# An attention layer and a routed expert layer on one core: two sends in flight, u before v, block 7's rotation after the experts

## The chip, the cores and the metric

One core of a Trainium2 chip runs the whole program. The metric is the device time of one launch in microseconds (us): three runs before, with a median of 402.08 (401.18 to 405.04). A profile was taken of one more execution.

## The reference

The input x has 8 batches (here called blocks, b = 0 to 7) of 512 rows of 128 numbers. Both branches read the normalized rows xn, and their results are added to x.

```python
xn = layernorm(x)                                   # outer one, without weights
# attention branch: its own layernorm on xn, with weights, gives y
uv = silu(y @ uv_w.T + uv_b); u, v, base = uv[..., :256], uv[..., 256:512], uv[..., 512:]
q, k = rope(base * gamma + beta)                    # two versions of base, each rotated
kernel = square(relu(q @ k.T / sqrt(128) + bias[distance]))
attn = (u * (kernel @ v)) @ o_w.T + o_b + xn
# expert branch: 4096 rows, 8 experts, each row goes to its best 2
probs = sigmoid(xn @ W_router); top 2, divided by their sum
ffn = sq_relu(xn @ W_sh_up) @ W_sh_down + sum over the 2 experts of weight * sq_relu(xn @ W_up[e]) @ W_down[e]
out = x + attn + ffn
```

## The kernel before, in words

Five engines run programs of their own and meet at semaphores; each executes its instructions in the order written. **Blocks 0 to 6** run first, one `turn` each, then the **experts**, then **block 7** by one more `turn`, then the results of the experts are added to all blocks (`combine`) and stored. A float32 product of full precision is made of three faster ones: each operand is split in a high half (a copy in a rounded type, by ScalarE) and a low half (the difference, by VectorE), and `product` (lines 1009 to 1011) multiplies low by high, high by low and high by high.

A turn of TensorE holds, for its block: v (`v_part`, four products of 256 columns for each half), two of the four parts of the shared expert's first layer (`shared_up`), the gate products u (`uv_part` by `gates`), the scores (`scores`, four), the other two shared parts, the shared second layer (`shared_down`), `values` (kernel times v, four), and among them the output product and the transposition of the block before (`output`, `output_turned`), and the transposed rows and the base products of the block after. In block 0 the gates come first and v last.

**Banks.** These products share a ring of four PSUM banks. `RING` lists its users in the order in which TensorE issues them, and `ring_free` makes TensorE wait until the user four places earlier has been read out. What counts as read out stands in `READ`: for v that VectorE has added v's bias, for u that ScalarE has applied SiLU (`u_silu`, line 495), for a shared part ScalarE's ReLU, for a score VectorE's first pass of the kernel square (line 782). In blocks 1 to 7 u's two banks are those that v's two halves had.

**VectorE's turn** (line 815): the gating u * (kernel @ v) of the block before (`gate`, line 793), `v_bias` (line 773), `qk_split` (line 767), four kernel squares (lines 782 and 785), the next block's norm, then the low halves and the rotation of the next block: `rotate_base` (lines 753 and 756) needs ScalarE's base_qk (line 482), `rotate_sum` (line 762) adds the two products. **ScalarE's turn** (line 513): first it waits for the rotated sum and copies its high half (qk_hi, line 515); then come the shared ReLUs, `v_silu` (line 490), `u_silu`, the squares, and the next block's base. `u_silu` also waits until the gating of the block before has read u.

**Routing.** In blocks 0 and 1 the rows of all eight groups are transposed (`routing_turned`), copied by ScalarE (`routing_copied`, line 455) and multiplied by the router's weights (`routing_logits`). Group g's logits wait for its copy. VectorE picks the two best in block 1, and in block 2 counts and places the rows (`routing_counts`, `routing_slots`). At the end of block 1 it makes the weights of the two experts (`routing_weights`, lines 703 to 709).

**Sends.** From block 2 on GpSimd issues 64 indirect DMAs (line 987), each of which writes 128 rows of 130 numbers to the slots of their experts in DRAM (`slots_in`). `IN_FLIGHT` is the number of semaphores (lanes) that they use in turn: a send waits for the landing of the send that had its lane before. SP loads W_up during the blocks (line 359), then W_down (line 370), then waits for all sends (line 374), and loads the slots' rows in pairs of tiles (line 378). There are 72 tiles of 128 slots. TensorE starts the experts when block 6 is added up (`mixed`) and the first pair of tiles has landed; the steps are paced by TensorE and results go back by GpSimd (line 996). Block 7 starts on TensorE when VectorE has made the last tile's result (line 911).

Of the kernel before, what the change touches and what calls it, by code (L numbers as in the profile page):

```python
# [67 lines left out]
def build(nc, x, ln_w, ln_b, uv_w, uv_b, gamma, beta, w, o_w, o_b,  # L68
# [10 lines left out]
    with ExitStack() as ctx:  # L79
# [111 lines left out]
        ld_w = [sem(f"ld_w{i}") for i in range(ROUNDS)]  # L191
        ld_wdn = sem("ld_wdn")
        zero_filled = sem("zero_filled")
        IN_FLIGHT = 2 * TOPK
        tokens_sent = [sem(f"tokens_sent{k}") for k in range(IN_FLIGHT)]
        zeros_set = sem("zeros_set")

# [52 lines left out]
        RING = [("x1", 0), ("x2", 0), ("base", 0), ("bsw", 0), ("rt", 0)]  # L250
        for b in range(B):
            values, up, gates, rt = [("v0", b), ("v1", b)], [("sh0", b), ("sh1", b)], [("u0", b), ("u1", b)], [("rt", g) for g in range(B)]
            if b == 0:
                RING += gates + up + values
            elif b == 1:
                RING += values + [rt[5], up[0], rt[6], up[1]] + gates + [rt[7]]
            else:
                RING += values + up + gates
            RING += [("qk0", b), ("qk1", b), ("qk2", b), ("qk3", b), ("sh2", b), ("sh3", b)]
            RING += [("fin", b - 1)] if 0 < b < LAST else []  # L260
            if b == 0:
                RING += [rt[1], ("x2", 1), rt[2], ("base", 1), ("bsw", 1), rt[3], ("x1", 1), rt[4]]
            elif b < LAST:
                RING += [("x2", b + 1), ("base", b + 1), ("bsw", b + 1), ("x1", b + 1)]
            if b >= LAST - 1:
                RING += [("fin", b)]
# [137 lines left out]
        def _(act):  # L404
# [46 lines left out]
            def routing_copied(g):  # L451
                act.wait_ge(ring_ready, ready("rt", g))
                if g >= 2:
                    act.wait_ge(logits_made, g - 1)
                act.copy(route_xt[g % 2].rearrange("p t d -> p (t d)"), ring("rt", g)[:, :]).then_inc(rx_copied, 1)
# [29 lines left out]
            def v_silu(b):  # L485
                for n in range(2):
                    act.wait_ge(v_biased, START + b * 2 + (n + 1))
                    act.wait_ge(av_done, START + b * TB)
                    part = vf[:, 2 * n:2 * n + 2, :].rearrange("p t e -> p (t e)")
                    act.activation(v[:, 2 * n:2 * n + 2, :].rearrange("p t e -> p (t e)"), part, ACT.Silu).then_inc(v_made, 1)  # L490

            def u_silu(b):
                act.wait_ge(g_made, START + b * 2)
                for n in range(2):
                    act.activation(ut[:, n, :], of_ring(f"u{n}", b), ACT.Silu, bias=uvbias[:, n:n + 1])\
                       .then_inc(ut_made, 1)
# [6 lines left out]
            def shared_square(b, c):  # L503
                act.wait_ge(sh_relu, START + b * HC + (c + 1))
                act.activation(sh[:, c % 2, :], sh[:, c % 2, :], ACT.Square).then_inc(sh_made, 1)
# [7 lines left out]
            def turn(b, first, last, route):  # L513
                act.wait_ge(qk_made, START + b + 1)
                act.copy(qk_hi[:, :, :].rearrange("p a t -> p (a t)"),
                         rot1.rearrange("p a t -> p (a t)")).then_inc(qk_hi_made, 1)
                if route == 1:
                    routing_copied(5)
                shared_relu(b, 0)
                if route == 1:  # L520
                    routing_copied(6)
                shared_relu(b, 1)
                v_silu(b)
                if not first:
                    u_silu(b)
                if route == 1:
                    routing_copied(7)
                shared_square(b, 0)
                shared_square(b, 1)
                if 0 < b < LAST:  # L530
                    output_out(b - 1)
                if route == 1:
                    routing_probs()
                if 3 <= route < LAST:
                    weights_hi(2 * route - 5)
                    weights_hi(2 * route - 4)
                shared_relu(b, 2)
                shared_relu(b, 3)
                if route == 0:
                    norm(1)  # L540
                    norm(2)
                    routing_copied(1)
                if not last:
                    second_rows_hi(b + 1)
                shared_square(b, 2)
                shared_square(b, 3)
                if route == 0:
                    norm(3)
                    norm(4)
                    routing_copied(2)  # L550
                if not last:
                    base_silu(b + 1)
                    if route == 0:
                        routing_copied(3)
                    first_rows_hi(b + 1)
                if route == 0:
                    routing_copied(4)
                    norm(5)
                    norm(6)
                    norm(7)  # L560
# [46 lines left out]
        def _(dve):  # L607
# [156 lines left out]
            def qk_split(b):  # L764
                dve.wait_ge(qk_hi_made, b + 1)
                dve.wait_ge(qk_made, START + b + 1)
                dve.tensor_tensor(qk_lo[:, :, :], rot1, qk_hi[:, :, :].bitcast(F32), ALU.subtract).then_inc(qk_lo_made, 1)  # L767
# [20 lines left out]
            def gate(b):  # L788
                dve.wait_ge(out_acc, START + b)
                for n in range(2):  # L790
                    dve.wait_ge(av_done, START + b * TB + TB)
                    dve.wait_ge(ut_made, START + b * 2 + (n + 1))
                    dve.tensor_tensor(g[:, n, :], P_AV[n][:, :], ut[:, n, :], ALU.mult).then_inc(g_made, 1)
# [21 lines left out]
            def turn(b, first, last, route):  # L815
                if 0 < b < LAST:
                    gate(b - 1)
                v_bias(b)
                qk_split(b)
                if route == 0:  # L820
                    statistics(2, 12, 20)
                    dve.wait_ge(ld["bias"], 16)
                kernel_square(b, 0)
                kernel_square(b, 1)
                if route == 0:
                    variances(slice(FIRST, 20))
                elif not last:
                    second_norm(b + 1)
                kernel_square(b, 2)
                kernel_square(b, 3)  # L830
                if route == 0:
                    second_norm(1)
                    statistics(3, 20, NT)
                if route == 1:
                    routing_first()
                if route == 2:
                    routing_counts()
                if route == 3:
                    routing_owners()
                if 3 <= route < LAST:  # L840
                    weights_lo(2 * route - 5)
                if not last:
                    second_rows_lo(b + 1)
                if 0 < b < LAST:
                    mix(b - 1)
                if route == 0:
                    variances(slice(20, NT))
                if route == 1:
                    routing_second()
                if route == 2:  # L850
                    routing_tiles()
                    routing_slots()
                if 3 <= route < LAST:
                    weights_lo(2 * route - 4)
                if not last:
                    rotate_base(b + 1)
                    first_rows_lo(b + 1)
                    rotate_sum(b + 1)
                if route == 1:
                    routing_weights()  # L860

            first_norm(0)
            second_norm(0, True)
# [61 lines left out]
            expert_steps(dve, step)  # L925


            turn(LAST, False, True, LAST)
            for b in (0, 1, 2):
                combine(b)  # L930
# [72 lines left out]
        def _(pe):  # L1003
# [132 lines left out]
            def turn(b, first, last, route):  # L1136
# [4 lines left out]
                def first_up():  # L1141
                    pe.wait_ge(x1_lo_made, START + b + 1)
                    if first:
                        pe.wait_ge(w_lo_made, 1)
                    shared_up(b, 0)
                    if route == 1:
                        routing_turned(6)
                    shared_up(b, 1)

                if first:  # L1150
                    gates()
                    first_up()
                v_part(b, 0)
                v_part(b, 1)
                if first:
# [1 line left out]
                    pe.wait_ge(ld["wr"], 16)  # L1157
                    routing_logits(0)
                if route == 1:
                    routing_logits(4)  # L1160
                    routing_turned(5)
                if not first:
                    first_up()
                    gates()
                if route == 1:
                    routing_logits(5)
                    routing_turned(7)
                    routing_logits(6)
                if route == 2:
                    routing_counted()  # L1170
# [147 lines left out]
```

## Time and profile before

| | us |
|---|---|
| median of 3 runs | 402.08 |
| profiled execution, own time | 402.41 |
| its span | 400.6 |
| mean granted TensorE clock | 0.977 |
| TensorE / ScalarE / VectorE / GpSimd busy | 366.8 / 238.3 / 230.9 / 154.0 |

The span begins with the first instruction and ends with the last; the own time holds what lies around it too. Blocks 0 to 6 take about the first 210 us, the experts end at 371, and block 7 and the sums take the rest. All times named below are counted from the span's start. A line of a timeline has start, duration, engine, source line, operation, what is written and read, how many such instructions follow one another, and in brackets how long the engine had been idle and whose result ended that. The bank names of TensorE have no numbers, and `work` holds many buffers: the source line tells which is meant.

### The profile page before, as it was taken

The page shows a single profiled execution, that of the slowest core. Times are in us where ns is not written, and L with a number is a line of the kernel's source. Part 1 is how long each engine was busy: PE and PEld are TensorE (multiplying, and loading weights), DVE is VectorE, ACT ScalarE, POOL GpSimd, SP SyncE. Part 2 cuts the span into 40 slices and gives each one's busy share as a digit, 9 for nine tenths or more (in the row PEclk, how much of TensorE's full clock was granted, in tenths as well). Part 3 has the DMA queues.
Part 4 walks back from the last instruction along what each step waited for, and adds up shares of the span by engine and source line. Part 5 has one row for each costly group of instructions (what it writes and reads, how often), then busy time and mean ns, then how long its engine had stood idle before and what let it go on. Part 6 is the DMA issues. An engine that isn't in the chain of part 4 may idle for free.

```text
span 400.6 us, 7289 instructions
## 1 busy us (share of the span) xinstructions
PE 366.8 (92%) x1966; PEld 278.8 (70%) x1967; DVE 230.9 (58%) x594; ACT 238.3 (59%) x447; POOL 154.0 (38%) x155
## 2 busy tenths in 40 slices
PE   1779899969989999999968999999999999999991
PEld 1565586556555656656526999999999999999740
DVE  3888458778986867858562333334334334333676
ACT  0765994752565746666434666666666676676420
POOL 3004600000277877776500344444444434445100
PEclk9989999989999999999996999999999999999997
DMA  6999000000012122156111122222222222221596
GB/s 158 316 291 272 15 2 0 0 2 0 7 47 82 58 80 75 47 145 209 49 27 28 55 56 60 67 60 60 65 62 60 58 62 66 62 64 33 152 298 200
DMA packets 50594, 34.53 MB, mean 86 GB/s; under 512 B 6032, under 2 KB 46864, under 8 KB 50576
## 3 DMA queue, kind: packets, MB, share of 16 engines
q1 hardware_dynamic: 44256, 23.77, 23.5%
q0 software_dynamic: 4352, 8.99, 6.7%
q10 hardware_dynamic: 1968, 1.55, 1.2%
q8 instruction: 9, 0.15, 0.2%
q14 instruction: 9, 0.07, 0.1%
HBM read 17.83 MB, written 16.47 MB: 86 GB/s over the span
## 4 chain that ended last, share of the span: by engine, by line
PE 72%; DVE 11%; ACT 9%; issue 4%; DMA 2%; ACTq 1%; POOL 0%; DVEq 0%; SPq 0%
PE bank L1281 16%; PE bank L1009 10%; PE bank L1010 9%; PE bank L1011 9%; PE bank L1262 8%; PE bank L1103 8%; PE bank L1089 4%; ACT base_qk L482 4%; PE bank L1109 3%; PE bank L1255 2%; PE bank L1066 2%; DVE work L756 2%; ACT work L477 1%; DVE qk_lo L767 1%; DVE work L762 1%
## 5 line engine op out<-in xcount | busy, mean ns | idle before, releaser
L996 POOL DMA_INDIRECT results<-work,dest x72 | 68.9, 958 | 106.3 <-DVE work L911 104.5
L987 POOL DMA_INDIRECT slots_in<-work,slot_i x64 | 69.9, 1092 | 79.3 <-issue 77.4
L1281 PEld LDWEIGHTS bank<-wdn,work 128*128 128x128 f32 x576 | 75.1, 191 | 6.0
L1281 PE MATMUL bank<-wdn,work 128*128 x576 | 75.7, 274 | 0.0
L911 DVE TENSOR_SCALAR work<-bank,row_sum 128x128 f32<-128x128 f32 x72 | 25.2, 350 | 83.7 <-PE bank L1281 83.7
L1103 PE MATMUL bank<-kern,v 128*128 128x512 f32 x128 | 58.7, 593 | 0.0
L592 ACT ACTIVATE work<-bank 128x512 f32<-128x512 f32 x72 | 43.2, 600 | 15.3 <-PE bank L1262 15.3
L598 ACT ACTIVATE work<-bank 128x512 f32<-128x512 f32 x72 | 43.1, 598 | 8.9 <-PE bank L1011 3.5
L1262 PE MATMUL bank<-cst,work 128*128 128x128 f32 x288 | 44.0, 276 | 0.0
L586 ACT CAST sx_hi<-bank 128x128 fp32r<-128x128 f32 x72 | 19.0, 266 | 31.4 <-PE bank L1255 31.4
L1103 PEld LDWEIGHTS bank<-kern,v 128*128 128x128 f32 x128 | 22.7, 190 | 20.6 <-issue 20.6
L1009 PE MATMUL bank<-wup_lo,sx_hi 128*128 x72 | 35.5, 493 | 0.7 <-DVE sx_lo L902 0.7
L501 ACT ACTIVATE work<-bank 128x512 f32<-128x512 f32 x32 | 18.8, 598 | 26.8 <-PE bank L1089 22.8
L1262 PEld LDWEIGHTS bank<-cst,work 128*128 128x128 f32 x288 | 34.0, 143 | 0.9 <-issue 0.4
L1089 PE MATMUL bank<-work,shdn 128*128 128x512 f32 x64 | 30.1, 593 | 0.0
L782 DVE SCALAR_TENSOR_TENSOR kern<-bank,bias_t 128x512 f32<-128x512 f32 x32 | 21.9, 684 | 13.2 <-PE bank L1011 13.2
L1010 PE MATMUL bank<-wup_hi,sx_lo 128*128 x72 | 29.1, 404 | 0.0
L1011 PE MATMUL bank<-wup_hi,sx_hi 128*128 x72 | 28.9, 402 | 0.0
L902 DVE TENSOR_TENSOR sx_lo<-bank,sx_hi 128x128 fp32r<-128x128 f32 x72 | 20.9, 291 | 9.9 <-ACT sx_hi L586 6.4
L785 DVE SCALAR_TENSOR_TENSOR kern<-kern 128x512 f32<-128x512 f32 x32 | 22.2, 693 | 1.1
L1255 PE MATMUL bank<-cst,slot_x 128*128 128x128 f32 x72 | 20.4, 286 | 2.0 <-issue 1.8
L1009 PE MATMUL bank<-x_lo,uvw_hi 128*128 128x512 f32 x32 | 15.7, 490 | 6.0 <-DVE work L773 4.4
(162 smaller groups left out, 652.2 us busy)
## 6 DMA issues: line engine op xcount, KB each, us to landing
slots_in<-zeros SPq DMA_DIRECT2D x1, 4752.0 KB, 22.2
slot_x<-slots_in SPq DMA_DIRECT2D x36, 132.0 KB
work<-in_L_ffn_W_up SPq DMA_DIRECT2D x8, 256.0 KB, 3.2
wdn<-in_L_ffn_W_down SPq DMA_DIRECT2D x4, 512.0 KB, 7.0
wup_hi<-results SPq DMA_DIRECT2D x8, 256.0 KB, 5.0
wup_lo<-results SPq DMA_DIRECT2D x8, 256.0 KB, 5.2
out<-x_all SPq DMA_DIRECT2D x8, 256.0 KB, 3.1
results<-work,dest POOLq DMA_INDIRECT x72
```

Of the source, the lines that this page charges most:

```text
L592: act.activation(hid_t[:, h, :], P_HT[h][:, :], ACT.Square).then_inc(hid_t_made, 1)
L598: act.activation(hid[:, h, :], P_UP[h][:, :], ACT.Relu).then_inc(relu_done, 1)
L987: pool.indirect_dma_start(slots_in, bass.IndirectOffsetOnAxis(slot_i[:, k, t:t + 1], 0), xs1[:, t, at], None, element_offset=k * 2).then_i ...
L996: pool.indirect_dma_start(results, bass.IndirectOffsetOnAxis(dest[:, at:at + 1], 0), slot_y[:, k, :], None).then_inc(returned[k], 16)
L1009: pe.matmul(dst, w_hi, m_lo, start=start, stop=False)
L1010: pe.matmul(dst, w_lo, m_hi, start=False, stop=False)
L1011: return pe.matmul(dst, w_hi, m_hi, start=False, stop=stop)
L1089: pe.matmul(P_OUT[:, :], shdn[:, c, :], sh[:, c % 2, :], start=(c == 0), stop=False).then_inc(shdn_done, 1)
L1103: last = pe.matmul(P_AV[e][:, :], v[:, j, e * P:(e + 1) * P], kern[:, j, :], start=(j == 0), stop=(j == TB - 1))
L1255: pe.transpose(P_SX[j % 2][:, 0:P], slot_x[:, g, j % 2, X0:X0 + D], ident).then_inc(sx_turned, 1)
L1262: last = pe.transpose(P_HT[h][:, c * P:(c + 1) * P], hid[:, h, c * P:(c + 1) * P], ident)
L1281: last = pe.matmul(P_Y[h][:, 0:D], hid_t[:, h, rows], wdn[:, of, c, :].rearrange("p a d -> p (a d)"), start=(c == 0), stop=(c == HC - 1))
```

## The change

- `IN_FLIGHT` goes from 4 lanes to 2, so that a send waits for the last but one.
- TensorE's turn is in the order u, shared parts 0 and 1, v, scores for all blocks, and `RING` follows. v's two halves now have the banks that u had. In block 1 the routing's transposes and logits are placed anew between them.
- ScalarE's turn has `u_silu` right behind the qk_hi copy, and `v_silu` behind the shared ReLUs.
- VectorE's turn has `qk_split` ahead of `v_bias`. `routing_weights` moves from the end of block 1 to block 2, behind `v_bias`.
- Block 7's `rotate_base` and `rotate_sum` move on VectorE from block 6 to behind the expert loop. ScalarE's part of them (base_qk) stays in block 6.

```diff
-        IN_FLIGHT = 2 * TOPK
+        IN_FLIGHT = TOPK
...
-            if b == 0:
-                RING += gates + up + values
-            elif b == 1:
-                RING += values + [rt[5], up[0], rt[6], up[1]] + gates + [rt[7]]
-            else:
-                RING += values + up + gates
+            RING += gates + ([rt[5], up[0], rt[6], up[1], rt[7]] if b == 1 else up) + values
...
                          rot1.rearrange("p a t -> p (a t)")).then_inc(qk_hi_made, 1)
+                if not first:
+                    u_silu(b)
...
                 shared_relu(b, 1)
-                v_silu(b)
-                if not first:
-                    u_silu(b)
                 if route == 1:
                     routing_copied(7)
+                v_silu(b)
...
                     gate(b - 1)
+                qk_split(b)
                 v_bias(b)
-                qk_split(b)
+                if route == 2:
+                    routing_weights()
...
+                if b < LAST - 1:
+                    rotate_base(b + 1)
                 if not last:
-                    rotate_base(b + 1)
                     first_rows_lo(b + 1)
+                if b < LAST - 1:
                     rotate_sum(b + 1)
-                if route == 1:
-                    routing_weights()
...
+            rotate_base(LAST)
+            rotate_sum(LAST)
             turn(LAST, False, True, LAST)
...
                     if route == 1:
                         routing_turned(6)
+                        routing_logits(5)
                     shared_up(b, 1)
-                if first:
-                    gates()
-                    first_up()
+                gates()
+                if route == 1:
+                    routing_logits(4)
+                    routing_turned(5)
+                first_up()
+                if route == 1:
+                    routing_turned(7)
                 v_part(b, 0)
                 v_part(b, 1)
...
                 if route == 1:
-                    routing_logits(4)
-                    routing_turned(5)
-                if not first:
-                    first_up()
-                    gates()
-                if route == 1:
-                    routing_logits(5)
-                    routing_turned(7)
                     routing_logits(6)
```

## Rows read from the trace of the kernel before

**Rows 1.** Page of the profile: each engine's busy time (part 1), all lines but TensorE's left out.

```profile
PE 366.8 (92%) x1966; PEld 278.8 (70%) x1967; DVE 230.9 (58%) x594; ACT 238.3 (59%) x447; POOL 154.0 (38%) x155
```

**Rows 2.** Timeline of TensorE, block 2: start us, us, what [idle before, releaser].

```profile
85.68 0.80 PE L1009 MATMUL bank<-x_lo,uvw_hi 128*128 128x512 f32 x1 [3.14 <-DVE work L773]
...
86.70 0.63 PE L1011 MATMUL bank<-x_hi,uvw_hi 128*128 128x512 f32 x1
...
89.24 0.58 PE L1009 MATMUL bank<-qk_lo,qk_hi 128*128 128x512 f32 x1
```

**Rows 3.** Timeline of VectorE, end of block 1 and start of block 2.

```profile
81.99 0.70 DVE L703 MEMSET wdn<- 128x768 f32 x1
...
83.75 1.28 DVE L793 TENSOR_TENSOR g<-bank,work 128x512 f32<-128x512 f32 x2
...
84.95 1.28 DVE L773 TENSOR_TENSOR work<-bank,vb_bc 128x512 f32<-128x512 f32 x2
```

**Rows 4.** Timeline of TensorE, blocks 1 and 4: first score, first v, first score.

```profile
59.70 0.48 PE L1009 MATMUL bank<-qk_lo,qk_hi 128*128 128x512 f32 x1
...
133.00 0.68 PE L1009 MATMUL bank<-uvw_lo,x_hi 128*128 128x256 f32 x1
...
138.09 0.50 PE L1009 MATMUL bank<-qk_lo,qk_hi 128*128 128x512 f32 x1
```

**Rows 5.** Timeline of ScalarE, block 1.

```profile
54.40 1.06 ACT L515 CAST qk_hi<-work 128x1024 fp32r<-128x1024 f32 x1
...
58.30 1.28 ACT L495 ACTIVATE work<-bank,uvbias 128x512 f32<-128x512 f32 x2
```

**Rows 6.** Timelines of VectorE and then ScalarE, block 0.

```profile
25.16 1.23 DVE L767 TENSOR_TENSOR qk_lo<-work,qk_hi 128x1024 fp32r<-128x1024 f32 x1 [0.74 <-ACT qk_hi L515]
...
36.54 1.65 ACT L444 ACTIVATE work<-x_all,shift,inv 128x128 f32<-128x128 f32 x4 [0.16 <-POOL shift L944]
```

**Rows 7.** Timeline of GpSimd, the 64 sends: first, one of three late ones, last.

```profile
107.81 1.22 POOL L987 DMA_INDIRECT slots_in<-work,slot_i  x1 [59.09 <-issue]
...
181.40 1.28 POOL L987 DMA_INDIRECT slots_in<-work,slot_i  x1 [0.46 <-DMA slots_in<-work,slot_i]
...
196.88 0.96 POOL L987 DMA_INDIRECT slots_in<-work,slot_i  x1 [0.30 <-issue]
```

**Rows 8.** DMA issues (last number: median us to landing) at 188:198, 176:182, 123.6, 169.1.

```profile
slots_in<-work,slot_i POOLq DMA_INDIRECT x8, 2.3
...
slots_in<-work,slot_i POOLq DMA_INDIRECT x5, 5.4
...
slots_in<-work,slot_i POOLq DMA_INDIRECT x1, 3.8
...
slots_in<-work,slot_i POOLq DMA_INDIRECT x1, 3.4
```

**Rows 9.** Chain of waits, one load of slot rows in the experts.

```profile
236.69 3.15 DMA slot_x<-slots_in
```

**Rows 10.** Timelines around the experts' start: VectorE, ScalarE, TensorE.

```profile
204.31 1.22 DVE L762 TENSOR_TENSOR work<-work 128x1024 f32<-128x1024 f32 x1
...
205.44 1.28 DVE L793 TENSOR_TENSOR g<-bank,work 128x512 f32<-128x512 f32 x2
...
202.43 0.57 ACT L471 CAST x_hi<-bank 128x512 fp32r<-128x512 f32 x1
...
211.41 0.54 PE L1255 MATMUL bank<-cst,slot_x 128*128 128x128 f32 x2 [1.81 <-issue]
```

**Rows 11.** Timeline of TensorE, first matmul after a gap in blocks 0 and 3.

```profile
26.44 0.50 PE L1009 MATMUL bank<-qk_lo,qk_hi 128*128 128x512 f32 x1 [1.87 <-DVE qk_lo L767]
...
112.70 0.50 PE L1009 MATMUL bank<-x_lo,uvw_hi 128*128 128x512 f32 x1 [1.29 <-DVE work L773]
```

**Rows 12.** Timeline of TensorE, block 7: first v, first score.

```profile
371.18 0.38 PE L1009 MATMUL bank<-uvw_lo,x_hi 128*128 128x256 f32 x1 [0.44 <-DVE work L911]
...
375.46 0.39 PE L1009 MATMUL bank<-qk_lo,qk_hi 128*128 128x512 f32 x1
```

## The prediction

> **What bounds the kernel now.** The engine totals of the page come first: TensorE is busy for 92% of the span [rows 1], so only its idle stretches and the stretches at half clock can be won. Its timeline shows where those are. Before block 2's gate products it waits 3.14 us for VectorE's v bias and then takes 0.63 us for a product matmul that takes 0.39 elsewhere [rows 2, 12]: the half clock. Before the output product of block 6 it waits again for the gating, which starts at 205.44, and the experts' first transposes come at 211.41 [rows 10]. Inside blocks 4 to 6 it has next to nothing to lose: 5.09 us from the first v matmul to the first score [rows 4], of which idle is under 0.3. The GpSimd timeline comes last, because it holds a second chain that TensorE's idle time doesn't name: 64 sends from 107.81 to 196.88 [rows 7]; the last lands 2.3 later, at 199.2 [rows 8], and only then are the experts' rows loaded (3.15 us a load [rows 9], done by about 202.4). So this chain now has 9 us to spare before 211.41.
>
> **Block 0.** v's bias (1.2 for the two halves) used to fill VectorE's 0.74 us wait for ScalarE's copy; now it comes after the 1.23 us qk_lo [rows 6], and statistics, kernel squares and variances come 1.2 later. TensorE hides that, GpSimd's shift doesn't: ScalarE's second norm already waits for it (0.16 [rows 6]), and of the 1.2 ScalarE's 0.6 us of idle a little further on absorbs half. From there ScalarE runs without a pause until block 1's qk_hi at 54.40 [rows 5]. Cost **+0.5**.
>
> **Block 1.** Two gate SiLUs (1.28 [rows 5]) now stand between qk_hi and the routing copy of group 5. TensorE's order puts the logits of group 5, which need that copy, ahead of the second shared product: copy done at 57.1, then logits 0.8, shared product 0.7, transposes 0.45, v 1.45, logits 0.8: the scores start at 61.4 instead of 59.70 [rows 4]. Cost **+1.7**.
>
> **Block 2.** The routing weights (81.99 to 83.75 [rows 3]) leave the path. The gating then ends at 83.1 and not at 84.95. TensorE now holds v where it held u, and v's bank comes free when the first gate SiLU is done (0.7): v starts at 83.8, 1.45 later and after 0.5 of counting the scores, at 85.9 against 89.24 [rows 2]. qk_lo (83.1 to 84.3) is in time. Gain **-3.3**, the half clock included: the gap left is 1.5 us, and it is taken to keep the clock, as block 3's 1.29 did [rows 11]. The routing weights now delay block 2's first kernel square to 87.9, which is covered: it used to start at 90.3, and TensorE needs it only after output and two more scores.
>
> **Blocks 3 to 6.** One wait replaces another of the same length: gating plus one u SiLU (0.7) for gating plus one half of v's bias (0.67). What is won is the order behind it, since qk_lo no longer follows the bias: 0.1 to 0.15 a block, **-0.5** in sum. The slots are thus made 1.1 earlier (0.5 + 1.7 - 3.3), the sends start at 106.7, and block 6 ends 1.6 earlier.
>
> **Before the experts.** Without block 7's rotation the gating follows x1's low half (0.68 from ScalarE's 203.0 [rows 10]); it starts at 203.7 and not 205.44, so TensorE would be ready for the experts 1.7 + 1.6 = 3.4 earlier, at **208.0**.
>
> **The sends.** With two in flight a send waits for the one before the last. In quiet stretches two pitches are 2.53 (0.96 and 0.30 ahead of it, twice), a landing 2.3 [rows 8], and the wake-up is at most the 0.3 that stands ahead of every send [rows 7]: 0 to 0.07 a pair, 0 to 2 us over 31 pairs; I take 0, because nothing shows that the 0.3 comes on top. Under other traffic it is different. Seven sends between 123 and 170 take 2.8 to 4.4 (the first and last [rows 8]) and each now holds up the whole queue behind it, where two lanes of slack hid it: 6.3 in sum. While w_down's 2 MB come in, five sends take 5.4 at the median [rows 8], and even with four in flight GpSimd waited there (0.46 ahead of one send, and two more like it) [rows 7]. Two at a time at 5.4 make about four sends in a stretch that held eight: **+5.0**. Together 11.3; the last lands at 199.2 - 1.1 + 11.3 = 209.4. The load takes 2.2 to 3.15 (the ends: the gap from landing until the data of the first pair stopped, and the steady load [rows 9]); with 2.8 the experts start at **212.2**, and this, not TensorE's 208.0, comes last: **+0.8**. From both sides: 208.0 at best (-3.4); with 13 us of delay and a full load 213.9 (+2.5).
>
> A rule of the Trainium skill speaks for less. DMA: Bandwidth & Descriptors, section "Queues, rings and completion order", says that each DMA engine takes turns between queues, packet by packet; by that a 65 KB send beside the big load should lose little, and the sum would be that of the second rival below. The 5.4 us row speaks against it.
>
> **Block 7.** VectorE's last expert result ends at 371.1, since TensorE waits for it until 371.18 [rows 12]. Two products and the sum, three operations of 1.2 [rows 10], end at 374.8, ScalarE's qk_hi (1.0) at 375.85, and only behind it in ScalarE's order comes the first u SiLU, at 376.5. TensorE has done u and shared products at 374.05: **a new gap of 2.5 us**. v then takes 1.45, the scores start at 378.1 and not at 375.46 [rows 12]. All behind it is as dense as before: **+2.6**.
>
> **Sum.** 0.8 + 2.6 = 3.4 on the profiled execution's own time of 402.41 (span 400.6), which stands 0.3 above the median: **405.8**. The gains of blocks 2 to 6 (3.8) are spent on the sends.
>
> **Rivals.**
> - *The half clock in block 7 (slower).* The place is the new gap; the price is that of block 2, where after 3.14 us of idle time the half clock lasted from 85.68 to shortly before 89.24 [rows 2], 3.4 us at half the pace and so 1.7 lost. It decides if 2.5 us of idle is enough. For: in block 0 the clock fell shortly after a gap of 1.87 [rows 11]. Against: after block 3's 1.29 it stayed [rows 11]. Time 407.5; with the sends at their worst bound 409.2. Chance 0.32.
> - *Sends hidden (about even or slightly faster).* If fewer sends in flight make each faster, the landing is before 205 and TensorE's 208.0 decides: -3.4 + 2.6 = -0.8, 401.6. For: four sends were in the same queue when 5.4 was measured. Against: the send at 123.62 took 3.8 with short queues. Chance 0.18.
> - *Much faster.* Also block 7's gap would have to be absent, and the losses of blocks 0 and 1: -5 or more, 397. It needs u's SiLU to be off the path, and the order written out says otherwise. Chance 0.05.
> - *Nothing moves:* the effects cancel elsewhere, 402.4. Chance 0.05.
>
> **How the numbers follow.** The forecast (404 to 406.6) has 0.40. The range takes in the hidden sends at the lower end and the half clock with late sends at the upper: 401.2 to 408.6. A measurement can tell about 1% (4.0 us) from no change. Slower by over 1% (above 406.1): the first rival and a fifth of the forecast, 0.40. Faster by over 1%: 0.07. Within 1%: 0.53.
>
> **What would show it.** Sends that wait for a send's landing in about 15 places instead of 3, the last started near 207; the first expert transpose at 211 to 213, waiting for the slot rows and not for the mix; TensorE idle for about 1.5 before block 2's v, 2.5 before block 7's v, released by ScalarE's line 495; block 1's scores 1.7 to 2.2 later. Wrong would be: an expert start before 209, no gap in block 7, or a half clock there.

## The result and the profile after

The changed kernel took 407.04 us in the median of 20 runs (401.96 to 412.85) against 402.00 for the kernel before, 5.0 us more. Six of the 20 (408.59 and above) count as slow and are left out of the ratio, although the clock of four of them, 0.974, is also that of a run that was kept. Without them it is **1.0098 [1.0066, 1.0129]**, about 4 us slower. The profiled execution is one of its faster ones: 404.05 us, span 402.2.

TensorE's waits after, from the list of who waited for whom (us in total, times, longest):

```profile
PE bank L1008 <- ACT work L490: 5.6, 6, 2.3
PE bank L1251 <- DMA slot_x<-slots_in: 2.8, 1, 2.8
PE bank L1036 <- ACT wdn L450: 2.1, 3, 1.0
PE bank L1008 <- DVE qk_lo L762: 2.0, 1, 2.0
```

VectorE's v bias (line 773 before) is gone from the list. In its place stand ScalarE's u SiLU (line 490 now) and the load of the slots' rows, for which TensorE waited 0.2 before. The other timeline lines of TensorE, with the idle time and its releaser in brackets, in the order block 1, block 2, experts, block 7:

```profile
56.78 0.63 PE L1065 MATMUL bank<-cst,work 128*128 128x128 f32 x4 [0.97 <-ACT work L490]
57.73 1.06 PE L1036 MATMUL bank<-wr,wdn 128*128 128x8 f32 x8 [0.32 <-ACT wdn L450]
...
63.67 0.48 PE L1008 MATMUL bank<-qk_lo,qk_hi 128*128 128x512 f32 x1
```

```profile
87.82 0.39 PE L1008 MATMUL bank<-uvw_lo,x_hi 128*128 128x256 f32 x1 [1.37 <-ACT work L490]
...
90.03 0.58 PE L1008 MATMUL bank<-qk_lo,qk_hi 128*128 128x512 f32 x1
```

```profile
207.25 0.66 PE L1115 MATMUL bank<-cst,work 128*128 128x128 f32 x4 [0.78 <-ACT work L506]
210.67 0.69 PE L1251 MATMUL bank<-cst,slot_x 128*128 128x128 f32 x2 [2.76 <-DMA slot_x<-slots_in]
```

```profile
369.68 0.50 PE L1008 MATMUL bank<-x_lo,uvw_hi 128*128 128x512 f32 x1 [0.44 <-DVE work L908]
...
374.98 0.39 PE L1008 MATMUL bank<-uvw_lo,x_hi 128*128 128x256 f32 x1 [2.27 <-ACT work L490]
...
376.50 0.40 PE L1008 MATMUL bank<-qk_lo,qk_hi 128*128 128x512 f32 x1
```

Against [rows 2, 4]: from block 1's first score to block 2's there are 26.4 us and not 29.5, and the gap of 3.14 is one of 1.37. Against [rows 12]: 6.8 us from block 7's first matmul to its first score and not 4.3, with a new gap of 2.27. Block 1's scores start 4.0 later than in [rows 4]. The experts start 0.7 earlier than in [rows 10], and the wait that ends last there is the load of the rows.

GpSimd's waits after, then its first and last send, and the median landing while W_down comes in (compare [rows 7, 8]):

```profile
POOL slots_in L986 <- issue: 64.8, 19, 59.3
...
POOL slots_in L986 <- DMA slots_in<-work,slot_i: 26.1, 45, 2.9
```

```profile
108.62 1.22 POOL L986 DMA_INDIRECT slots_in<-work,slot_i  x1 [59.30 <-issue]
...
206.04 0.96 POOL L986 DMA_INDIRECT slots_in<-work,slot_i  x1 [0.32 <-DMA slots_in<-work,slot_i]
```

```profile
slots_in<-work,slot_i POOLq DMA_INDIRECT x3, 5.8
```

Of the 64 sends 45 now wait for a landing, 3 did before; in 14 of the 45 the idle time is 0.4 or more, where 0.3 stands ahead of every send. They take 97.4 us from first start to last start where they took 89.1, and with the 2.3 of a landing the rows' loads can begin at 208.3 and not at 199.2.

### The profile page after: what moved, and what is told of

The parts are those of the page before. It is cut to its first block, busy times and chain, and to the rows that moved or that the text cites. A ratio compares the mean times of both kernels' runs of the same rounds, so it can differ in the third digit from the quotient of the medians.

```text
span 402.2 us, 7288 instructions
## 1 busy us (share of the span) xinstructions
PE 365.9 (91%) x1966; PEld 278.1 (69%) x1967; DVE 232.0 (58%) x594; ACT 239.6 (60%) x447; POOL 150.9 (38%) x155
## 4 chain that ended last, share of the span: by engine, by line
PE 46%; DMA 20%; issue 18%; POOL 6%; DVE 6%; ACT 2%; SPq 0%; DVEq 0%; ACTq 0%; POOLq 0%
DMA slots_in<-work,slot_i 18%; PE bank L1277 16%; PE bank L1258 8%; PE bank L1008 6%; PE bank L1009 5%; PE bank L1010 5%; POOL slots_in L986 4%; POOL inv L939 2%; PE bank L1251 2%; PE bank L1102 2%; DMA x_all<-in_L_attn_x 1%; DVE x_all L808 1%; DVE x_all L806 1%; PE bank L1065 1%; ACT base_qk L477 1%
## 5 line engine op out<-in xcount | busy, mean ns | idle before, releaser
L986 POOL DMA_INDIRECT slots_in<-work,slot_i x64 | 66.8, 1043 | 90.9 <-issue 64.8
L1088 PEld LDWEIGHTS bank<-work,shdn 128*128 128x128 f32 x64 | 12.0, 189 | 11.7 <-issue 11.0
```

Of the source, the lines that this page charges most:

```text
L986: pool.indirect_dma_start(slots_in, bass.IndirectOffsetOnAxis(slot_i[:, k, t:t + 1], 0), xs1[:, t, at], None, element_offset=k * 2).then_i ...
L1088: pe.matmul(P_OUT[:, :], shdn[:, c, :], sh[:, c % 2, :], start=(c == 0), stop=False).then_inc(shdn_done, 1)
```

## The experiments

Each change is made to the kernel named; ratios are to the kernel before on the same chip, with 95% intervals. "After" is the changed kernel.

### Two lanes against four

**a_four_lanes** (after): `IN_FLIGHT = 2 * TOPK`.

> The changed kernel with four sends in flight again, nothing else. Theory (the sends decide when the experts start): GpSimd no longer waits outside of the W_down load, the last send lands about 8 us earlier (near 200), the first expert transpose waits for the mix at 207.9 + 1.1 = 209 and not for the slot rows; 1.7 us of the 210.67 are won, the 2.3 us gap before block 7's v stays. Time 0.4% below the changed kernel, ratio to the kernel before 1.005. Rival (two lanes cost nothing, the loss is in the order): ratio stays 1.01.

Measured **0.9997 [0.9963, 1.0032]**.

```profile
210.42 0.69 PE L1251 MATMUL bank<-cst,slot_x 128*128 128x128 f32 x2 [1.80 <-issue]
```

```profile
374.97 0.39 PE L1008 MATMUL bank<-uvw_lo,x_hi 128*128 128x256 f32 x1 [2.29 <-ACT work L490]
```

The expert transpose waits for "issue" again, with 1.80 idle as in [rows 10], the gap in block 7 stays. The lanes alone thus cost the change about 1.0% (this ratio against 1.0098, on another chip), 4 us give or take 2, where I expected 1.7 from its profiled execution. A likely reason is in two other two-lane profiles below: their sends ended later than that execution's. The sends of unprofiled runs can't be seen. That the transpose comes at 210.42 and not at 209 is block 1 again: from block 0's first score to block 1's there are 37.8 us here, 37.1 in the changed kernel.

**b_two_lanes** (before): `IN_FLIGHT = TOPK`.

> The kernel before with two sends in flight alone. Theory: the sends take 8 to 9 us longer (100 instead of 91), the last lands near 207.5, and the slot rows are there at about 209.8, 1.6 ahead of the 211.41 at which the mix lets TensorE start: no change, ratio 1.000 to 1.004. Rival (the landings get longer as well, 11 us as forecast): rows at 212.5, ratio 1.003 to 1.006.

Measured **1.0038 [1.0004, 1.0073]**; single times 401.4 to 407.7. The profiled one:

```profile
109.43 1.22 POOL L987 DMA_INDIRECT slots_in<-work,slot_i  x1 [60.50 <-issue]
...
208.40 0.96 POOL L987 DMA_INDIRECT slots_in<-work,slot_i  x1 [0.31 <-issue]
```

```profile
214.52 0.49 PE L1255 MATMUL bank<-cst,slot_x 128*128 128x128 f32 x2 [3.18 <-DMA slot_x<-slots_in]
```

The ratio lies in both ranges (up to 1.004 and from 1.003). The profile has what only the rival holds: the last send lands at 212.2, and the experts wait until 214.5. From the first send to the last landing two lanes took 99.7 (after), 103.5 (a_rotation_back) and 102.8 (here), four lanes 89.4 to 91.4 in seven profiles. The loss by the ratio (1.5 us) is smaller than this execution's (4.1); the medians of all times, 405.27 and 402.37, are 2.9 apart. So other executions probably land earlier, which no trace shows.

**a_wdown_after** (after; what it changes is when W_down is loaded):

```diff
+            for lane in range(IN_FLIGHT):
+                sp.wait_ge(tokens_sent[lane], 16 * TOPK * NT // IN_FLIGHT)
             for e in range(0, NE, 2):
                 sp.dma_start(wdn[:, e:e + 2], ...).then_inc(ld_wdn, 16)
-            for lane in range(IN_FLIGHT):
-                sp.wait_ge(tokens_sent[lane], 16 * TOPK * NT // IN_FLIGHT)
```

> The changed kernel with the load of W_down issued behind the last send's landing instead of beside the sends; its experts start late for that, only the sends count. Theory (of the 8.4 us by which two lanes stretch the sends, some 4 to 5 are paid while W_down comes in): from first send to last landing 95 us instead of 99.7, no send over 4 us late in the last third. Rival (two lanes cost a little in every pair): 99 us or more.

**a_wdown_after2**, the same kernel.

> The kernel of a_wdown_after again for the same reason. Same expectation: from first send to last landing 95 us instead of 99.7 if W_down's load is what stretches them; 99 or more if every pair pays a little.

Both ran on a chip on which the kernel before took 441 us, so their times (464 and 415) say nothing. The traces from that chip have no landings; with 2.3 taken for the last one, first send to last landing took 86.5 us in the first (107.36 to 191.54) and 99.0 in the second:

```profile
109.54 1.22 POOL L986 DMA_INDIRECT slots_in<-work,slot_i  x1 [59.31 <-issue]
...
206.25 0.96 POOL L986 DMA_INDIRECT slots_in<-work,slot_i  x1 [0.30 <-issue]
```

The first goes beyond the theory's 95, the second meets the rival's 99. But the first had less traffic: TensorE stood still for 15.6 us and then for 30.9, and SP's loads of W_up, which keep pace with the blocks, came late:

```profile
191.57 0.58 PE L1008 MATMUL bank<-uvw_lo,x_hi 128*128 128x256 f32 x1 [30.86 <-issue]
```

Two of these loads of 256 KB were issued beside its sends (at 125.7 and 143.5, the next at 207.1), and six beside those of the second and of the changed kernel. With so little beside them two lanes cost nothing in that execution. In the second, 28 sends waited 17.5 us in all for landings (8.4 of it is the usual 0.3) with W_down out of the way, so it can't be W_down alone; what the W_up loads have in it was not tried by itself.

### Block 7's rotation

**a_rotation_back** (after): the last two lines of VectorE's diff undone, the rotation of block 7 in block 6.

> The changed kernel with block 7's rotation back in block 6, two lanes kept. Theory: the gap of 2.3 us before block 7's v goes, and the 1.7 us by which TensorE is ready later for the experts are hidden by the sends, which end the wait in any case (210.67); so the whole 2.5 us is won and the ratio falls to about 1.003. Rival (the early gating is worth something): TensorE's readiness decides, experts start 1.7 later, net win 0.8, ratio 1.008.

Measured **1.0018 [0.9990, 1.0046]**.

```profile
213.34 0.69 PE L1247 MATMUL bank<-cst,slot_x 128*128 128x128 f32 x2 [4.89 <-DMA slot_x<-slots_in]
```

```profile
371.91 0.50 PE L1004 MATMUL bank<-x_lo,uvw_hi 128*128 128x512 f32 x1 [0.44 <-DVE work L906]
...
376.19 0.40 PE L1004 MATMUL bank<-qk_lo,qk_hi 128*128 128x512 f32 x1
```

First matmul to first score of block 7: 4.3 us again, no gap. TensorE waits 4.89 for the rows, so in this execution the early gating is worth nothing, as expected. Against the changed kernel's 1.0098 this is 3.2 us, give or take 1.7, where 2.5 was expected.

**b_rotation_late** (before): only the rotation moved behind the experts.

> The kernel before with block 7's rotation alone moved behind the experts; v before u, four lanes. Theory: the gating of block 6 starts 1.7 us earlier and the experts with it (the sends have 9 us to spare), but block 7's scores then wait for qk_lo: rotation 3.6, qk_hi 1.05, v's bias 1.3 and qk_lo 1.2 behind VectorE's last expert result, so they start 7.2 us after it instead of 4.3; net 1.2 lost, ratio 1.003. Rival (the early gating is worth more than the gap): ratio 0.996 or less.

Measured **1.0006 [0.9967, 1.0046]**, which separates neither.

```profile
209.62 0.43 PE L1259 MATMUL bank<-cst,slot_x 128*128 128x128 f32 x2 [1.80 <-issue]
```

```profile
367.86 0.39 PE L1013 MATMUL bank<-uvw_lo,x_hi 128*128 128x256 f32 x1 [0.44 <-DVE work L913]
...
372.09 0.50 PE L1013 MATMUL bank<-x_lo,uvw_hi 128*128 128x512 f32 x1 [1.15 <-DVE work L773]
...
373.83 0.50 PE L1013 MATMUL bank<-qk_lo,qk_hi 128*128 128x512 f32 x1
```

Its trace shows both halves of the bargain: experts at 209.6 (1.8 earlier), block 7's scores 6.0 us behind its first matmul (1.7 more). My 7.2 was wrong by counting v's bias behind the rotation in full: it runs while ScalarE makes qk_hi.

**a_silu_first** (after): in ScalarE's turn for block 7, `u_silu(b)` ahead of the wait for the rotated sum.

```diff
             def turn(b, first, last, route):
+                if last:
+                    u_silu(b)
                 act.wait_ge(qk_made, START + b + 1)
...
-                if not first:
+                if not first and not last:
                     u_silu(b)
```

> The changed kernel (two lanes), with block 7's two u SiLUs ahead of ScalarE's wait for the rotated sum instead of behind the qk_hi copy; blocks 1 to 6 as they were. Theory (the 2.3 us gap before block 7's v is ScalarE's order: the SiLU that frees v's bank stands behind the rotation): v follows the shared products with no gap over 0.3; now the first score waits, for qk_lo, which needs rotation 3.6, qk_hi 1.0 and 1.2 of splitting behind the last expert result, and starts 5.9 to 6.0 us behind it instead of 6.9. Won 0.9, ratio about 1.008. Rival (the gap is VectorE's, v's bank is late for another reason): gap and time unchanged, ratio 1.010.

**a_silu_first2**, the same kernel.

> The kernel of a_silu_first again, since there the kernel before took 441 us as well and no time could be read. Same expectation: no gap before block 7's v, first score 5.9 to 6.0 us behind the last expert result instead of 6.9, 0.9 won, ratio about 1.008; rival 1.010 with the gap as it was.

Here too the kernel before took 441 and 442 us, and the ratio (0.93) isn't used. The order inside block 7 can be read; VectorE and then TensorE, second run (the first gives the same distance):

```profile
377.78 0.35 DVE L910 TENSOR_SCALAR work<-bank,row_sum 128x128 f32<-128x128 f32 x1 [0.98 <-PE bank L1279]
...
382.84 1.23 DVE L764 TENSOR_TENSOR qk_lo<-work,qk_hi 128x1024 fp32r<-128x1024 f32 x1 [1.11 <-ACT qk_hi L512]
```

```profile
378.19 0.50 PE L1010 MATMUL bank<-x_lo,uvw_hi 128*128 128x512 f32 x1 [0.78 <-DVE work L910]
...
381.06 0.28 PE L1010 MATMUL bank<-uvw_lo,x_hi 128*128 128x256 f32 x1
...
384.12 0.50 PE L1010 MATMUL bank<-qk_lo,qk_hi 128*128 128x512 f32 x1 [1.47 <-DVE qk_lo L764]
```

v (381.06) follows the shared products without a gap, and the first score waits 1.47 for qk_lo. It starts 6.0 us behind the last expert result, against 6.9 in the changed kernel. So the gap before v is ScalarE's order. The 1.5 that TensorE now waits for qk_lo is the price of the late rotation itself, which this order doesn't remove.

### The order, and the routing weights

**b_order** (before): u, shared, v with its bank, SiLU and bias orders; four lanes, routing weights and rotation where they were.

> The order alone: u, shared, v, with v's bias behind qk_lo and the u SiLU behind the qk_hi copy; four lanes, routing weights at the end of block 1, block 7's rotation in block 6. Theory: block 0 loses 0.5, block 1 2.2 and 1.7 more where its gaps bring the half clock; block 2 keeps a gap of about 3.2 us with the half clock, 0.1 to 0.15 a block is won in blocks 3 to 6. Sum +2 to +4, ratio 1.005 to 1.010. Rival (the order is what gained in block 2): ratio at or below 1.000.

Measured **1.0085 [1.0059, 1.0112]**.

```profile
88.91 0.58 PE L1004 MATMUL bank<-uvw_lo,x_hi 128*128 128x256 f32 x1 [3.33 <-ACT work L490]
```

The big gap is still there, now behind the u SiLU: the order didn't remove it. By itself the order costs 3.4 us, give or take 1.1, within what was expected here and twice what the prediction's terms for it give (0.5 + 1.7 - 0.5 = 1.7). With the routing weights (-3.1, next run) that is about even for blocks 0 to 6, where the prediction had a gain of 1.6.

**b_weights_moved** (before):

```diff
                 v_bias(b)
                 qk_split(b)
+                if route == 2:
+                    routing_weights()
...
-                if route == 1:
-                    routing_weights()
```

> The kernel before with the routing weights alone moved from the end of block 1 to block 2, behind v's bias and qk_lo, four lanes, all else as before. Theory (the routing weights caused the 3.14 us gap): the gap shrinks by 1.76 to 1.4 us, TensorE keeps the full clock there (worth 1.7 more), block 2's scores start near 86, the experts 3.3 earlier, ratio 0.992. Rival (the order u before v did it): gap unchanged, ratio 1.000.

Measured **0.9922 [0.9891, 0.9954]**.

```profile
83.72 0.50 PE L1009 MATMUL bank<-x_lo,uvw_hi 128*128 128x512 f32 x1 [1.19 <-DVE work L773]
...
85.90 0.58 PE L1009 MATMUL bank<-qk_lo,qk_hi 128*128 128x512 f32 x1
```

Gap 1.19, first matmul behind it at full pace (0.50), scores at 85.9 against 89.24: the gain is that of the routing weights.

### Putting it together

**a_four_rot_gap** (after, four lanes):

```diff
             gate(LAST - 1)
+            rotate_base(LAST)
             mix(LAST - 1)
+            rotate_sum(LAST)
...
-            rotate_base(LAST)
-            rotate_sum(LAST)
             turn(LAST, False, True, LAST)
```

> The changed kernel with four lanes, and block 7's rotation put into VectorE's idle time around the mix of block 6: gating, two products, mix, sum. Theory: both costs of the change go; the early gating stays, the rotation is hidden ahead of the experts, no gap before block 7's v. Against the changed kernel 1.7 + 2.5 less, ratio to before 0.999. Rival (VectorE delays the mix or the first expert rows): experts 1 us later, ratio 1.002.

Measured **0.9918 [0.9879, 0.9958]**, better than expected: 7.2 us below the changed kernel for 4.2. It fits the single runs, by which the lanes cost 4.1 and the late rotation 3.2.

**best** (before, with the routing weights' and this rotation's place, and nothing else).

> The kernel before (v before u, four lanes) with the routing weights in block 2 and block 7's rotation around the mix of block 6. Theory: 3.3 from block 2 and 1.7 from the early gating, nothing lost elsewhere; ratio 0.988. Rival (the gains are taken back because the sends then decide): they start 3.3 earlier too, so the slack is still 7 us; if it isn't, ratio 0.994.

Measured **0.9864 [0.9822, 0.9907]**, 396.4 us. VectorE around the mix:

```profile
199.53 1.28 DVE L793 TENSOR_TENSOR g<-bank,work 128x512 f32<-128x512 f32 x2
200.73 1.21 DVE L753 TENSOR_TENSOR work<-base_qk,cos_sin 128x1024 f32<-128x1024 f32 x1
201.86 1.22 DVE L756 TENSOR_TENSOR work<-base_qk,cos_sin 128x1024 f32<-128x1024 f32 x1
203.00 0.68 DVE L799 TENSOR_TENSOR x_all<-x_all,work 128x512 f32<-128x512 f32 x1
203.78 0.69 DVE L802 TENSOR_TENSOR x_all<-bank,x_all 128x512 f32<-128x512 f32 x1
204.39 1.21 DVE L762 TENSOR_TENSOR work<-work 128x1024 f32<-128x1024 f32 x1
```

```profile
205.55 0.43 PE L1259 MATMUL bank<-cst,slot_x 128*128 128x128 f32 x2 [1.86 <-issue]
```

The rotation fits between gating and mix (where VectorE had been idle) and behind the mix; TensorE starts the experts 5.9 us earlier than in [rows 10]. Sends end at 195.1, loads follow by about 2.3, so 8 us of slack remain.

## Why the prediction was right, point by point

The time and its direction were right (405.8; 1.0098 on the median of 402.0 is 405.9), and so was the mechanism: the sends decide when the experts start, and block 7 gets a gap. Two terms on the way were off, in opposite directions: block 1's, and the sends' stretch in the profiled execution. By its own steps:

- **Block 0, +0.5:** right. ScalarE's second norm waits 1.72 for GpSimd's shift instead of 0.16, and block 1's qk_hi comes 0.6 later than in [rows 5]:

```profile
37.87 1.65 ACT L439 ACTIVATE work<-x_all,shift,inv 128x128 f32<-128x128 f32 x4 [1.72 <-POOL shift L943]
...
55.00 1.05 ACT L510 CAST qk_hi<-work 128x1024 fp32r<-128x1024 f32 x1
```

- **Block 1, +1.7:** the order's cost is right, its consequence was missed. In a_rotation_back the scores come 35.6 us behind block 0's first score, 33.3 before: 2.3, as 0.5 + 1.7. In the changed kernel's trace it is 37.1: behind the two gaps (0.97, 0.32) the granted clock was half from 59.3 to 62.7. First a_rotation_back's score, then the changed kernel's clock (the last but two of the numbers):

```profile
62.42 0.48 PE L1004 MATMUL bank<-qk_lo,qk_hi 128*128 128x512 f32 x1
```

```profile
55.00:59.00 4.00, 2.71 (x19) 1.99 (x18) 1.23 (x1) 3.64 (x7) 0.00 (x0) 1.00 0.00 0
59.40:62.70 3.30, 3.30 (x16) 3.19 (x15) 0.69 (x1) 1.21 (x3) 0.00 (x0) 0.50 0.02 5
```

  I had weighed the half clock for block 7's new gap and not for these; it costs 1.6 here. This term of the sum was mis-sized, and it makes block 6 end level with before instead of 1.6 earlier.
- **Block 2, -3.3:** right, -3.2 with a gap of 1.37 for 1.5, and by b_weights_moved for the stated reason. The half clock stayed away.
- **Blocks 3 to 6, -0.5:** right, -0.55 in sum from score to score.
- **Before the experts:** TensorE's transposes of block 6 come at 207.25. With the 2.5 us that lay between them and the first expert transpose before (208.94 to 211.41) it would have been ready at about 209.7; forecast 208.0, late mainly by the 1.6 of block 1.
- **Sends:** first at 108.6 (forecast 106.7), stretched by 8.4 (11.3), last landing 208.3 (209.4), experts 210.7 (212.2). In a_rotation_back and b_two_lanes the stretch was 12.2 and 11.4, so the size was fair and the profiled execution is at the lucky end. Luck is also that its sends started 1.9 later than forecast and were stretched 2.9 less, which nearly cancels. Of the stretch the part under W_down's load came out as forecast: three sends start between 176.3 and 186.5, while it comes in, where seven did before (176.0 to 186.6; forecast four for eight), and four pitches are 5.1 (5.0). The other late sends cost 3.3 for 6.3. The 14 sends that idle for 0.4 or more are the "about 15 places" of the prediction. That sends decide was right: without two lanes the ratio is 0.9997. The upper bound of 213.9 was added up with a load of 2.8; with the full 3.15 that it names it is 214.25. By the rule of the Trainium skill that the prediction names (DMA: Bandwidth & Descriptors, "Queues, rings and completion order": each DMA engine takes turns between queues, packet by packet) a send would lose little beside the big load; three of them took 5.8 at the median here, so this case's trace doesn't bear that out.
- **Block 7, +2.6:** right: 6.88 from last expert result to first score against 4.33, gap 2.27 for 2.5, on ScalarE's line as said, at full clock. VectorE's last expert result, before and after:

```profile
370.78 0.35 DVE L911 TENSOR_SCALAR work<-bank,row_sum 128x128 f32<-128x128 f32 x1 [0.65 <-PE bank L1281]
```

```profile
369.27 0.35 DVE L908 TENSOR_SCALAR work<-bank,row_sum 128x128 f32<-128x128 f32 x1 [0.65 <-PE bank L1277]
```

  The first rival fell at its place; its mechanism struck in block 1. The second fell with a_four_lanes (the sends were not hidden, and didn't get faster by being fewer), the third with the gap in block 7.
- **Sum:** 3.4 forecast; 1.6 in the profiled execution (the experts' start is 1.5 earlier than forecast), 4 by the ratio of the runs. That their sends end later is the likely reason; besides the profiled execution only the two of the bullet on the sends show it.

## What to carry to other kernels

A reordering of three engines' programs is a bundle of separate bargains: here moving one short routine off the path won 0.8%, and the order (0.85% alone), the smaller number of transfers in flight (1.0%) and the displaced rotation (0.8% in the changed kernel) lost more than that together. A moved step belongs where its engine is idle, not behind the end of the path, and everything queued behind it on the next engine moves with it: the rotation's price was a bank held by an activation that didn't need it. Two transfers in flight cost nothing while two pitches cover one landing and the restart behind it; a later landing holds up all sends behind it. Look at the landings under other traffic, not at the quiet median.

## What the runs showed of the hardware

- A send starts 0.27 us behind the landing that frees its lane: the one at 181.40 in [rows 7] waited for the send of 175.73, which took 5.4. The shortest landings are 2.27; two lanes then just allow the 2.53 of two pitches, so quiet stretches cost nothing, as taken: the changed kernel's last sends start at 203.50, 204.76 and 206.04.
- Two gaps of together 1.3 us were followed by half clock (a granted clock of 0.50) in block 1 of the changed kernel, single gaps of 1.37, 1.40, 2.04 (block 0) and 2.27 us were not. Nine profiles have the new order in block 1 and the same two gaps: five show half clock behind them for 3.4 us (after, a_four_lanes, a_four_rot_gap, a_silu_first, a_wdown_after2), four don't. a_silu_first and a_silu_first2 are one kernel and differ in it. The gap of 2.04 in block 0 was followed by half clock in a_rotation_back. So the same gaps go either way from one execution to the next, and a gap's length alone didn't decide it here.
- On one chip TensorE, VectorE and ScalarE stood still for several us at a time in three of its four profiles (TensorE's 4.04 before 153.82 in a_silu_first2 and 30.86 before 191.57 in a_wdown_after have no releaser), while GpSimd's sends went on, and the kernel before took 441 us there. Why was not tried.
